# Macaron block with routed experts on one core: the experts' down product as three half-precision products, and the instruction orders planned anew

## The reference, cut to what matters

```python
# x: 16 sequences x 512 tokens x 256 channels, float32
x = x + 0.5 * ffn(layernorm(x))                 # pass "A"
x = x + attn(layernorm(x))                      # "T": time mix and scan over the tokens
x = x + 0.5 * ffn(layernorm(x))                 # pass "B", same weights as A

def ffn(x):                                     # E=8 experts, I=128, top 2 of 8
    shared = (silu(x @ ws_gate.T) * (x @ ws_up.T)) @ ws_down.T       # inner width 256
    scores = sigmoid(x @ gate_weight.T); topk_w, topk_idx = top_k(scores, 2)
    topk_w = topk_w / topk_w.sum(-1) * 2.5
    hmid = silu(x @ w_gate[e].T) * (x @ w_up[e].T)                   # per chosen expert
    return shared + sum_over_chosen(topk_w * (hmid @ w_down[e].T))

def attn(x):
    xx = x shifted by one token
    k, v, r = (x*m + xx*(1-m)) @ W.T            # for k, v, r
    state_t = k_t*v_t + exp(decay)*state_{t-1};  o_t = r_t*(first*k_t*v_t + state_t)
    return layernorm(o) @ Wo.T
```

## Time and profile before

| | us |
|---|---|
| median of 3 runs (lowest, highest) | 1133.9 (1128.15, 1135.17) |
| span of the profiled execution | 1279.5 |
| PE, DVE, POOL, ACT busy in it | 991.1, 788.2, 695.5, 412.1 |

### The profile page before, as it was taken

One profiled execution on the slowest core, in us unless ns is written; L12 is line 12 of the kernel. 1 busy time (PEld: TensorE's weight loads), 2 busy tenths in 40 slices (PEclk: granted clock), 3 DMA queues, 4 the chain that ended last, 5 costly groups with the idle time before them and its releaser, 6 DMA issues.

```text
span 1279.5 us, 23262 instructions
## 1 busy us (share of the span) xinstructions
PE 991.1 (77%) x7488; PEld 696.8 (54%) x7488; DVE 788.2 (62%) x2485; ACT 412.1 (32%) x737; POOL 695.5 (54%) x684
## 2 busy tenths in 40 slices
PE   2767986889957876989867899778787997877560
PEld 1434663565835544657755576456465675656450
DVE  5855554979655875875247697554587885324233
ACT  5332441445313532423213354112233533212110
POOL 2766445764156885274256334754667455355555
PEclk9888988999979887999878899888988999878875
DMA  8668689673266632337777535764876346679974
GB/s 241 203 182 165 131 217 201 141 177 105 66 150 140 152 99 87 79 103 188 170 166 179 132 83 106 175 188 134 208 154 164 94 92 185 163 184 246 225 194 139
DMA packets 337989, 198.58 MB, mean 155 GB/s; under 512 B 251728, under 2 KB 319952, under 8 KB 337872
## 3 DMA queue, kind: packets, MB, share of 16 engines
q1 hardware_dynamic: 312432, 129.84, 41.8%
q0 software_dynamic: 24576, 67.14, 20.6%
q10 hardware_dynamic: 864, 0.12, 0.1%
HBM read 47.05 MB, written 92.27 MB: 109 GB/s over the span
## 4 chain that ended last, share of the span: by engine, by line
PE 51%; issue 18%; DVE 11%; another core or an unknown queue 7%; POOL 6%; DMA 3%; ACT 2%; SPq 1%; ACTq 0%; POOLq 0%; DVEq 0%
PE ps L1029 11%; PE ps L962 10%; PE ps L922 5%; PE ps L924 5%; PE ps L926 5%; PE ps L1063 3%; PE ps L895 2%; PE ps L893 2%; PE ps L894 2%; POOL xsB L835 2%; DVE acc L1254 2%; PE ps L954 1%; POOL y_got L852 1%; PE ps L958 1%
## 5 line engine op out<-in xcount | busy, mean ns | idle before, releaser
L922 PE MATMUL ps<-xq,w_hi 128*128 128x128 f16 x1248 | 238.2, 231 | 45.2 <-issue 37.8
L926 PE MATMUL ps<-xq,w_lo 128*128 128x128 f16 x1248 | 239.1, 231 | 35.7 <-issue 35.6
L924 PE MATMUL ps<-xq,w_hi 128*128 128x128 f16 x1248 | 238.9, 231 | 29.5 <-issue 29.2
L1227 DVE SCALAR_TENSOR_TENSOR hid<-ps,hid 128x512 f32<-128x512 f32 x144 | 97.2, 678 | 220.2 <-remote 112.3
L962 PE MATMUL ps<-wd,hid 128*128 x624 | 175.1, 425 | 33.2 <-ACT y_sb L1146 11.2
L1129 ACT ACTIVATE hid<-ps 128x512 f32<-128x512 f32 x144 | 85.1, 591 | 328.1 <-remote 185.2
L852 POOL DMA_INDIRECT y_got<-ysB,y_pos x128 | 124.9, 975 | 99.3 <-DVE acc L1254 50.4
L835 POOL DMA_INDIRECT xsB<-rows,pos x128 | 131.6, 1028 | 79.3 <-DVE pos L1384 43.1
L835 POOL DMA_INDIRECT xsA<-rows,pos x128 | 132.1, 1032 | 74.2 <-DVE pos L1384 38.8
L1254 DVE SCALAR_TENSOR_TENSOR acc<-y_got,share,acc 128x256 f32<-128x256 f32 x256 | 127.8, 507 | 58.3 <-DMA y_got<-ysB,y_pos 31.2
L962 PEld LDWEIGHTS ps<-wd,hid 128*128 128x128 f32 x624 | 128.0, 213 | 65.4 <-issue 47.2
(11 more groups left out here) (138 smaller groups left out, 1804.4 us busy)
## 6 DMA issues: line engine op xcount, KB each, us to landing
ysA<-y_sb SPq DMA_DIRECT2D x36, 512.0 KB
ysB<-y_sb SPq DMA_DIRECT2D x36, 512.0 KB
acc<-in_x_dram SPq DMA_DIRECT2D x16, 512.0 KB
out_dram<-acc SPq DMA_DIRECT2D x16, 512.0 KB
xsA<-zeros SPq DMA_DIRECT2D x36, 128.0 KB
xsB<-zeros SPq DMA_DIRECT2D x36, 128.0 KB
acc<-in_w_chunks_dram SPq DMA_DIRECT2D x10, 256.0 KB, 4.7
xq<-xsA SPq DMA_TRANSPOSE x156
```

Of the source, the lines that this page charges most:

```text
L922: nc.tensor.matmul(half, w_hi[2 * k + b][:, cols], hi, start=(j == 0 and k == 0), stop=False, skip_group_check=True)
L924: nc.tensor.matmul(half, w_hi[2 * k + b][:, cols], lo, start=False, stop=False, skip_group_check=True)
L926: mm = nc.tensor.matmul(half, w_lo[2 * k + b][:, cols], hi, start=False, stop=(j == many - 1 and k == KC - 1), skip_group_check=True)
L1227: v.scalar_tensor_tensor(out=hid[:, i % N_HID, some], in0=ps[:, bank_of("gate_up", key, 1), some], scalar=W_UNSCALE, in1=hid[:, i % N_HID, ...
```

## The change

Three things. (1) The experts' down weights are split like the others (`wd_hi`, `wd_lo`, staged in `acc`), the gated values of *every* chunk are split by `hidden_hi` and `hidden_lo`, and `down` of an expert block is three half-precision matmuls; `evac` takes the factor 256 out again. (2) One ring of split pairs serves all chunks (`N_SPLIT` 2 to 3), and `hid` is free after `hidden_lo` (`N_HID` 4 to 3). (3) The planner's durations and all its tables and paces have other values; quads of a group may now come in any order (`opens_group`, `last_quad`), and a bias may be added out of turn. `E_GAP` and `EB_GAP` are negative, so each group's quads run from the last to the first.

```diff
-N_ROWS, N_XT, N_XQ, N_Y, N_HID, N_SPLIT = 3, 2, 4, 3, 4, 2
+N_ROWS, N_XT, N_XQ, N_Y, N_HID, N_SPLIT = 3, 2, 4, 3, 3, 3
...
-    T_LATER = (-3.2, 0.2, 12.0, -1.8, 3.6, 4.1, 2.4, 5.3, 12.6, -3.2, -4.1, -4.2, -6.1, -13.4, -5.3, -22.0)
+    T_LATER = (-71.3, 182.7, -215.7, -79.7, 481.5, -49.2, 595.8, -302.7, 840.1, -58.0, 514.0, 66.1, -53.3, 323.7, -39.5, 350.9)
...
-    PACE = 32.3
...
-    E_GAP = 6.2
-    EB_GAP = 8.4
...
+    PACE = 19.6
...
+    E_GAP = -18.4
+    EB_GAP = -12.3
...
-        if what == "S":
-            add("act", "hidden_hi", key, 0.63, at + 3, [("gated", key)])
-            add("dve", "hidden_lo", key, 0.72, at + 4, [("hidden_hi", key)])
-            add("pe", "down", key, 1.47, at + 5, [("hidden_lo", key)])
-        else:
-            add("pe", "down", key, 0.48 * blocks_of(f, a, b), at + 4, [("gated", key)])
+        add("act", "hidden_hi", key, 0.63, at + 3, [("gated", key)])
+        add("dve", "hidden_lo", key, 0.72, at + 4, [("hidden_hi", key)])
+        add("pe", "down", key, 1.47 if what == "S" else 0.33 * blocks_of(f, a, b), at + 5, [("hidden_lo", key)])
...
-                [("y_store", (f, g, QUADS[f, g] - 1)), ("y_places", (f, g))], lag=2.0)
+            add("pool", "gather", (f, s, h), 2.53, at + h,
+                [("y_store", (f, g, q)) for q in range(QUADS[f, g])] + [("y_places", (f, g))], lag=3.2)
...
-        wd = sb("wd", [P, 2, NE * P])
+        wd_hi = sb("wd_hi", [P, 2, NE * P], F16)
+        wd_lo = sb("wd_lo", [P, 2, NE * P], F16)
...
                     if what == "S":
...
+                        cols, w, w_rest = slice(which[1] * P, (which[1] + 1) * P), ws_hi, ws_lo
                     else:
-                        cols = bass.ds(expert_cols[key][j], P)
-                        mm = nc.tensor.matmul(half, hid[:, b, tok], wd[:, :, cols], start=(j % 2 == 0),
-                                              stop=(j % 2 == 1 or j == many - 1), skip_group_check=True)
+                        cols, w, w_rest = bass.ds(expert_cols[key][j], P), wd_hi, wd_lo
+                    nc.tensor.matmul(half, hid_h[:, n, tok], w[:, :, cols], start=(first and j % 2 == 0),
+                                     stop=False, skip_group_check=True)
+                    nc.tensor.matmul(half, hid_l[:, n, tok], w[:, :, cols], start=False, stop=False,
+                                     skip_group_check=True)
+                    mm = nc.tensor.matmul(half, hid_h[:, n, tok], w_rest[:, :, cols], start=False,
+                                          stop=(last and (j % 2 == 1 or j == many - 1)), skip_group_check=True)
...
+                if i >= N_SPLIT:
+                    act.wait_ge(down_done, i + 1 - N_SPLIT)
+                nc.scalar.copy(hid_h[:, i % N_SPLIT, some], hid[:, i % N_HID, some]).then_inc(hi_done, 1)
...
+                    if i > 1:
+                        ins = low(wd_lo[:, :, cols], wd_stage[:, :, cols], wd_hi[:, :, cols])
```

116 lines of the change are left out of this document (50 added, 66 removed).

## The result

| | before | after |
|---|---|---|
| median us (lowest, highest) | 1131.66 (1128.15, 1135.17), 4 runs | 1096.33 (1093.42, 1100.71), 4 runs |
| ratio after / before, 95% interval | | 0.9694 [0.9655, 0.9733] |
| span of the profiled execution | 1279.5, a second one 1133.5 | 1096.9, a second one 1092.0 |

The change takes 35 us off, 3.1%. The forecast was to take off 47 us. The execution of the kernel before that was profiled for the prediction was an unusual one (granted clock 0.891 where the timed runs of `before_again` have 0.931 to 0.945): profiled again, the same kernel spans 1133.5 us, as its timed runs do. From here on the kernel before is read from that second profile, and differences need no scaling.

A forecast was written before the change was run, and what follows sets the result against it. PE's products were taken to bound dense stretches, waits for scattered rows and stores the loose ones, POOL the tail. Terms -25 + 18 + 2 - 33 - 15 = -53 us, scaled by 0.886 to -47: 1087 us, range 1035 to 1145.

The forecast's parts named there:

- order, middle and head: Up to PE's last scan turn (head: before the first): fuller PE from the new order, -33 us before scaling.
- order, tail: Behind PE's last scan turn: ten gathers moved ahead of the last scatter, fewer blocks left; -15 us before scaling.
- down weights: First 60 us: splitting two loads of down weights on ACT and DVE, +2 us before scaling.
- The frame: Sum made against the profiled span of 1279.5 us, then scaled by 0.886 to the runs' median of 1133.9.
- The down product: Expert down on PE: 0.41 us less per quad, 36 us in all, 69% on the chain: -25 us before scaling.
- The splitting: `hidden_lo` on DVE for 80 expert chunks, 55 us, partly in dense places: +18 us before scaling; ACT hides `hidden_hi`.
- Rival 2: DVE takes PE's place between scan turns, gains of products and middle vanish: +27 us, 1161 us; chance 0.15.
- Rival 3: Work moved before the first scan turn gives back what the middle gains: 1134 us; chance 0.13.
- Rival 1: The new order is worth nothing, only PE's products count: -15 us, 1119 us; chance 0.17.
- The sign of 145 to 155 us: If the forecast is right, the time from the last scatter to the end is 145 to 155 us.
- Rival 4: The new `hidden_lo` on DVE holds POOL (GpSimd), 30 us more: 1114 us; chance 0.05.

The follow-up runs named there:

- before_again: The kernel before, unchanged, profiled and timed a second time: 1131.6 us, ratio 0.9989.
- new_order_f32: Kernel after with its lists, but expert down in float32, without the experts' `hidden_lo` and the split of down weights: 1081.8 us, ratio 0.9562 to before.
- two_products: Kernel after with two half-precision matmuls per expert block instead of three, `hidden_lo` still made: 1093.1 us, ratio 0.9667 to before.
- double_lo: Kernel after with every expert `hidden_lo` made twice: 1113.0 us, ratio 0.9828 to before.
- short_lo: Kernel after with the experts' `hidden_lo` on 16 of its columns only: 1088.2 us, ratio 0.9606 to before.
- no_lo: Kernel after without the experts' `hidden_lo`, the wait for it and the product of the rest: 1092.2 us, ratio 0.9622 to before.
- gathers_late: Kernel after with POOL's ten early gathers, and their combines on DVE, put behind the last scatter: 1113.7 us, ratio 0.9834 to before.
- all_f32: Kernel after with expert and shared down both in float32, no splitting of gated values or down weights: 1082.2 us, ratio 0.9551 to before.

## Why the prediction was right and where it was wrong

The total lies inside the range and on the right side: 1096 us against 1087 forecast. Its parts did less well; two errors of opposite sign (the products, the tail) cancelled in part, so that the total came this near is in part luck. In us of a run, forecast terms times 0.886:

| term | forecast | measured |
|---|---|---|
| order, middle and head | -29 | -27 (new_order_f32: 934.4 to 907.7) |
| order, tail | -13 | -27 in new_order_f32, -22 in after |
| order and rings together | -43 | -51 (by medians; -54 by the two spans) |
| products, splitting, down weights | -22 + 16 + 2 = -4 | +9 to +15 |

**The frame.** The scaling by 0.886 treated the long execution as a stretched picture of a normal one. It wasn't: its chain had PE at 51% where the second profile has 24%, and 7% of "another core or an unknown queue", of which the second has none. Why that execution took longer stays open. With 24% + 17% the products' term would have been 36 x 0.41 = -15 instead of -25, still far from what was measured.

**The down product: the step "only what lies on the chain counts: 69%" failed.** The price on PE was right: 1.31 us per quad in the timeline, and PE's busy time fell by 36 us (925.3 to 889.2), the upper bound given. What failed is the step from a share of the chain to a price. Three runs with the same lists and 34 us of PE less, as is, and more spread over 5 us. A share of the chain says for how much of the span an engine was the last one waited for; it is no rate at which its time is paid. Two things can take its place. The granted clock fell where products were taken away, which gave back some 12 of 34 us in two_products. And when PE's part is shortened, the next wait (turned rows, `kv_sb`, DVE's mixes) ends almost at the same moment; that is my reading of the waits, no run shows it.

**The splitting: the right size, rather too high.** +16 forecast. Doubling `hidden_lo` cost 17 us by medians and 15 to 21 by ratios, cutting it to 16 columns gave back 4 to 10. DVE's busy time rose by 46 us between the kernels; at the price of a saved us, 0.1 to 0.3, that is 5 to 14. DVE's busy time is 848.5, forecast 843; ACT's 456, forecast 462. That the chunk's longer chain would be covered was right: PE's waits for `hidden_lo` come to 3.1 us in the whole span after, where before's second profile has 19.1 us, with only 64 shared chunks. The smaller ring of `hid`, costed at nothing, does show: ACT's silu waits 14.4 us for `hidden_lo` in five waits. PE's own waits for silu stay at 1.5 us.

**Rival 2** (DVE takes PE's place) holds in part. Its sign, DVE over 90% busy in most intervals between scan turns, was met: 9 of 15 (7 of 15 in the second profile, 3 of 15 in new_order_f32). DVE's time has a price of its own (double_lo) while PE's has nearly none. It did not eat the order's gain, as the rival said; it turned the products' gain into a loss of 9 to 15 us. Of this short_lo accounts for some half. What the rest is stays open: short_lo and no_lo have DVE's work of new_order_f32 in the middle (514 and 504 against 511.5 us), less on PE, and still take 5 to 7 us longer there. It isn't the splitting of the down weights, which lies in the head (318.6 in short_lo, 319.9 in new_order_f32). The granted clock (0.98 and 0.96 in the middle against 0.99) would fit, and it went along with PE's work in all ten measurements; the register instruction per block would fit too. Neither was tried alone.

**The order, middle.** It was taken at half of what filling the gaps could give, -29 in a run, and came out at -27 with the float32 down and at -14 with the three products, which took the rest back. The signs are there: the longest interval fell to 76 us, the first scan turn came 89 us later (75 forecast), the last one 14 us earlier. Rival 3 (the head gives back what the middle gains) was the right thing to fear: of the 104 us that the middle lost, 89 stand in the head. Rival 1 (the order is worth nothing) is wrong.

**The tail** was mis-sized: -13 forecast, from ten gathers at 1.25 us and little else; measured -22 and -27. gathers_late prices those ten gathers with their combines at 16 to 21 us, since the step counted POOL's own time and not the combines behind them. The step also took the waits before the gathers from the whole kernel of an execution that is not the usual one, 63.5 us for `combine`; before's second profile has 2.4 us of them in the tail, and 24.1 us of waits for the stores of expert rows instead. These fell to 12.9 us after, and to 0.9 in new_order_f32, whose waits for `combine` are longer (16.9 us) instead. The forecast named PE's smaller tail (70 blocks instead of 81) but gave it no price; that the expert work ends earlier against the gathers is how I read the shorter waits for stores. Last scatter to end is 127 us, 18 less than before. The sign of 145 to 155 us was given in the frame of the long execution, where before had 1279.5 - 1112.1 = 167; scaled by 0.886 it is 128 to 137, and 127 lies just below.

**Rival 4** was right that GpSimd and `hidden_lo` meet, and wrong about who pays in the long meetings (below). Its price of 30 us on POOL isn't there: POOL's busy time rose by 16 us. Some of that goes with `hidden_lo` all the same, for POOL is at 712 us in both profiles of after, at 698 to 703 in short_lo, new_order_f32 and no_lo, and at 693 in all_f32; but double_lo, with 80 more, has 711.

Of the kernels timed here the better one keeps the new order and leaves the down product in float32: new_order_f32 or all_f32, ratios 0.9562 and 0.9551, about 1% faster than the kernel after.

## What to carry to other kernels

An engine's share of the chain, or of the span, is no price for its time: here 81% busy and a price of up to 0.1, and a cheaper product on the busiest engine lost about 1%, some half of it since the splitting went to the second busiest. Before a change is costed from a profile, see whether the profiled execution is one of the usual ones; its own span against the runs tells it at a glance. Look at an engine's share interval by interval: joined stretches hid nine intervals with DVE above 90%. And time a new order apart from the new arithmetic: here the order, with its rings, gave all of the gain, and old tables under the planner's new settings gave a list slower than either.

## What the runs showed of the hardware

**A DVE subtraction is held by a GpSimd addition.** `hidden_lo` (two operands in SBUF) has its median at 684 ns, as in the earlier trace rows, but one instruction reaches 3287 ns. One line's instructions, kernel after:

```profile
L1227 DVE TENSOR_TENSOR hid_l<-hid,hid_h x144: 546/684/3287, 48.4 to 1060.6; 128x512 f16<-128x512 f32 x136, 128x384 f16<-128x384 f32 x8
```

Two are long in the timeline, and beside each stands POOL's bias (2.36 us, two operands in SBUF as well). The third pair is a `combine` (L1247, also two operands in SBUF) beside another bias:

```profile
491.62 2.36 POOL L857 TENSOR_TENSOR acc<-acc,o_bias 128x1024 f32<-128x1024 f32 x1
491.88 2.65 DVE L1227 TENSOR_TENSOR hid_l<-hid,hid_h 128x512 f16<-128x512 f32 x1
...
691.10 3.29 DVE L1227 TENSOR_TENSOR hid_l<-hid,hid_h 128x512 f16<-128x512 f32 x1
691.47 2.36 POOL L857 TENSOR_TENSOR acc<-acc,o_bias 128x1024 f32<-128x1024 f32 x1
...
856.45 3.24 DVE L1247 SCALAR_TENSOR_TENSOR acc<-y_got,share,acc 128x256 f32<-128x256 f32 x1
857.05 2.35 POOL L857 TENSOR_TENSOR acc<-acc,o_bias 128x1024 f32<-128x1024 f32 x1
```

The first ends 0.55 us after the bias ends (494.53 against 493.98), the second began 0.37 us before the bias and ended 0.56 us after it. Their excess, 1.97 + 2.61 = 4.6 us, is nearly all of the higher mean: 136 x (721 - 685) ns = 4.9 us. double_lo has one more such pair, 2.61 us beside the bias at 495.54. So it is DVE that was held, for the length of the bias, and the bias kept its 2362 ns in the mean in both kernels. Rival 4 had it the other way round.

It isn't new with this change, nor is it special to `hidden_lo`. A `combine` has a median of 485 ns and a longest of 3242 after and 3128 in the second profile of before, and both times a bias stands beside it. A gate product with one of its operands in PSUM (`hid<-ps,hid`) that began beside a bias at 422.92 in the second profile of before took its usual 0.69 us.

The Trainium skill (GPSIMD Engine Reference, Key points) speaks of contention between the two on the SBUF interfaces for DVE instructions with two SBUF inputs; this case agrees, with the pairs above. The gathers and scatters, which are short bookkeeping on POOL, show it little: a scatter's median is 967 to 974 ns with and without the change, and only its mean went from 1023 and 1031 to 1069 and 1058 (`xsB`, `xsA`).

**Columns of busy time of matmuls don't add.** In the groups by line (second profile of before, first of after) the expert down went from 156.6 us (624 records of 395 ns, shows their form) to three groups of 85.9 us, 258 together, while PE's busy time fell by 36. The records overlap; the distance between starts, 0.109 us, is the price.
